# Experts of a small mixture-of-experts layer summed feature-major instead of token-major, with routing coefficients spread through DRAM

## The reference, cut to what matters

```python
xn = layernorm(x)
logits = xn @ router_w + router_b + load_balancer          # 4 experts
rw, sel = top_k(logits, 2); rw = softmax(rw)
e0 = silu(xn @ sw_w1) * (xn @ sw_w3) @ sw_w2               # 128 -> 512 -> 128
e1 = gelu(sym(xn) @ me_c1w + me_c1b) @ me_c2w + me_c2b     # 128 -> 256 -> 128
h2 = layer_norm(syn + attn); ff = relu(h2 @ ce_f1w + ..) @ ce_f2w + ..
e2 = layer_norm(h2 + ff) @ ce_gen_w + ce_gen_b
e3 = gelu(xn @ ml_w1 + ml_b1) @ ml_w2 + ml_b2              # 128 -> 512 -> 128
out = x + attention(xn) + sum over the two chosen experts of rw * e
```

## Time and profile before

| | us |
|---|---|
| median of 3 runs | 510.76 (510.4 to 511.81) |
| the profiled execution | 510.39 |
| its span, first to last instruction | 508.3 |
| PE busy | 487.1 (96%) |
| DVE busy | 402.1 (79%) |
| ACT busy | 231.0 (45%) |
| POOL busy | 172.9 (34%) |

### The profile page before, as it was taken

How to read it: one execution, slowest core, us unless ns; L and a number is a source line. 1 busy time by engine, 2 the same in 40 slices (tenths; PEclk the granted TensorE clock), 3 DMA queues, 4 the chain that set the end, 5 groups by cost and what they waited for, 6 DMA issues and landing times.

```text
span 508.3 us, 9640 instructions
## 1 busy us (share of the span) xinstructions
PE 487.1 (96%) x3072; PEld 425.5 (84%) x3072; DVE 402.1 (79%) x1339; ACT 231.0 (45%) x413; POOL 172.9 (34%) x310
## 2 busy tenths in 40 slices
PE   3779999999999999999999999999999999999995
PEld 2559898898989889898988989898898989889894
DVE  5997886868788686878968687896868789695875
ACT  3452634626363462636346263634626363462621
POOL 5351433415243341524334152432415243240320
PEclk9989999999999999999999999999999999999998
DMA  6000001010100101010010101001010100100000
GB/s 244 3 1 21 3 1 43 2 43 0 43 0 0 41 0 41 0 41 0 0 41 0 41 0 41 0 0 41 0 41 0 41 0 0 41 2 23 0 22 21
DMA packets 17921, 11.21 MB, mean 22 GB/s; under 512 B 752, under 2 KB 17264, under 8 KB 17904
## 3 DMA queue, kind: packets, MB, share of 16 engines
q1 hardware_dynamic: 17616, 10.85, 7.1%
q10 hardware_dynamic: 288, 0.15, 0.1%
HBM read 6.80 MB, written 4.19 MB: 22 GB/s over the span
## 4 chain that ended last, share of the span: by engine, by line
PE 92%; DVE 5%; DMA 1%; issue 0%; ACT 0%; DVEq 0%; SPq 0%
PE EX L901 22%; PE S L935 12%; PE S L937 11%; PE S L936 11%; PE ATT L991 7%; PE EX L913 6%; PE S L944 5%; PE EX L921 3%; PE S L975 2%; PE S L1012 1%; PE S L1010 1%; PE S L1011 1%; DMA W<-weights 1%; PE TR L972 1%; PE S L1026 1%; PE TR L858 1%
## 5 line engine op out<-in xcount | busy, mean ns | idle before, releaser
L935 PE MATMUL S<-xh,WH 128*128 128x512 f32 x224 | 94.5, 422 | 2.5 <-DVE pr L724 1.8
L937 PE MATMUL S<-xh,WL 128*128 128x512 f32 x224 | 89.1, 398 | 0.0
L936 PE MATMUL S<-xl,WH 128*128 128x512 f32 x224 | 88.8, 396 | 0.0
L901 PEld LDWEIGHTS EX<-W,hid 128*128 128x128 f32 x512 | 59.7, 192 | 1.4
L401 POOL TENSOR_TENSOR hidl<-hid,hidh 128x512 fp32r<-128x512 f32 x32 | 40.8, 1295 | 56.8 <-ACT hidh L487 56.8
L901 PE MATMUL EX<-scaled,hid 128*128 128x128 f32 x512 | 59.8, 275 | 0.0
L901 PE MATMUL EX<-W,hid 128*128 128x128 f32 x512 | 59.8, 274 | 0.0
L901 PEld LDWEIGHTS EX<-scaled,hid 128*128 128x128 f32 x512 | 58.5, 192 | 0.1
L935 PEld LDWEIGHTS S<-xh,WH 128*128 128x128 f32 x224 | 42.4, 189 | 18.1 <-DVE gate L730 5.7
L361 POOL TENSOR_TENSOR veps_x<-mv_x,eps 128x4 f32<-128x4 f32 x16 | 3.3, 205 | 153.9 <-DVE mv_x L518 153.9
L652 DVE SCALAR_TENSOR_TENSOR OUT<-EX,coef,OUT 128x128 f32<-128x128 f32 x192 | 53.8, 344 | 1.3 <-PE EX L913 0.2
(11 more groups left out here) (166 smaller groups left out, 945.2 us busy)
## 6 DMA issues: line engine op xcount, KB each, us to landing
X<-x SPq DMA_DIRECT2D x16, 256.0 KB, 2.9
out<-OUT SPq DMA_DIRECT2D x16, 256.0 KB, 2.3
W<-weights SPq DMA_DIRECT2D x1, 768.0 KB, 9.2
W<-weights SPq DMA_DIRECT2D x1, 512.0 KB, 8.1
W<-weights SPq DMA_DIRECT2D x1, 418.5 KB, 7.3
W<-weights SPq DMA_DIRECT2D x1, 384.0 KB, 8.6
W<-weights SPq DMA_DIRECT2D x1, 320.5 KB, 8.1
ROW<-rows ACTq DMA_DIRECT2D x1, 133.0 KB, 5.3
```

The lines of the kernel that those rows point to most:

```text
L901: ins = pe.matmul(EX[EX_BANK[e]][:, t, :], hid[e][:, j, t * P:(t + 1) * P], weight[:, j * P:(j + 1) * P], start=(e == 0 and j == 0), stop= ...
L935: pe.matmul(bank[:, :], wh, hi, start=True, stop=False)
L936: pe.matmul(bank[:, :], wh, lo, start=False, stop=False)
L937: pe.matmul(bank[:, :], wl, hi, start=False, stop=True).then_inc(unit_ready, 1)
```

## The change

Expert results are now feature-major like the first products. Each second product (`expert`, `expert2`) is a float32r triple per 128 hidden features, so the weights sw_w2 (halved), me_c2w, ml_w2 and the folded gen_w are split too, and the hidden tiles of experts 0, 1 and 3 as well as u need high halves (ACT) and low halves (POOL for experts 3, 2 and 0, DVE for expert 1 and u). The `tok` tiles take a split form as well (TH, TL), eight matmuls with the high half of x, then four with its low half. The copy xT is gone.

A coefficient now belongs to a column, not to a partition. POOL computes the coefficients (`weigh`), SP writes them to DRAM (`kept`, 128 x 16 elements) and reads them back with every partition receiving all 2048 of them (`share`, 8 KB per partition, 1 MB). The inverse deviation of u times coefficient 2 goes the same way (`kept_u`, `share_u`, 2 KB per partition). DVE sums the experts in `acc`, 512 columns at a time, with the bias of an expert as a scalar per partition; PE turns acc back (`turn_back`), and one DVE operation adds it to OUT (`finish`). The ranking works in the bank TR with fewer semaphore steps.

```diff
+        acc = [sb(f"acc{k}", [P, T]) for k in range(2)]
+        share = [sb(f"share{k}", [P, P, NT, E]) for k in range(2)]
+        share_u = sb("share_u", [P, P, NT])
...
+            def spread_u(g):
+                sp.wait_ge(u_weighed, g.count(1, 1))
+                sp.dma_start(kept_u[g.par], u_weight[:, :]).then_inc(kept_u_stored, DMA_INC)
+                sp.wait_ge(kept_u_stored, g.count(DMA_INC, DMA_INC))
+                sp.dma_start(share_u[:, :, :], kept_u[g.par:g.par + 1].broadcast_to([P, P, NT])) \
+                    .then_inc(share_u_loaded, DMA_INC)
+            def spread(g):
+                sp.wait_ge(coef_ready, g.count(1, 1))
+                sp.dma_start(kept[g.par], coef[g.par][:, :, :].rearrange("p t e -> p (t e)")) \
+                    .then_inc(kept_stored, DMA_INC)
+                sp.wait_ge(kept_stored, g.count(DMA_INC, DMA_INC))
+                sp.dma_start(share[g.par][:, :, :, :].rearrange("p q t e -> p q (t e)"),
+                             kept[g.par:g.par + 1].broadcast_to([P, P, NT * E])).then_inc(share_loaded, DMA_INC)
             def turn(g, first, last):
                 if not first:
-                    store(g.prev())
+                    spread_u(g.prev())
+                spread(g)
                 if two_more(g):
                     sp.wait_ge(att_added, g.count(1, 1))
                     load_x(Group(g.pair, g.off + 2))
+                if not first:
+                    store(g.prev())
...
+            def weigh(g):
+                pool.wait_ge(tlean_ready, g.count(1, 1))
+                pool.tensor_tensor(turned[:, :, :], tlean[:, :, :], half[:, :, :], ALU.mult)
+                pool.drain()
+                pool.tensor_tensor(coef[g.par][:, :, :], turned[:, :, :], half[:, :, :], ALU.add) \
+                    .then_inc(coef_ready, 1)
...
-                pool.wait_ge(hid_high, g.count(1, 1))
-                for j in range(2):
-                    pool.tensor_tensor(hidl[:, j, :], hid[2][:, j, :], hidh[:, j, :], ALU.subtract) \
-                        .then_inc(hid_low, 1)
+                low(3, 0, 2)
+                low(3, 2, 4)
+                weigh(g)
+                low(2, 0, 2)
+                low(0, 0, 2)
+                low(0, 2, 3)
+                low(0, 3, 4)
...
-                act.copy(xT[g.par][:, :], TR[:, :])
                 act.copy(xh[g.par][:, :], TR[:, :]).then_inc(x_high, 1)
...
                 half_gate(1)
+                high(3, 0, 2, "c1")
+                high(3, 2, 4, "c3")
...
+            def scale(g, n, e):
+                dve.wait_ge(ex_ready, g.count(E, n))
+                bank = EX[EX_BANK[e]][:, :, :]
+                dve.scalar_tensor_tensor(out=bank, in0=bank, scalar=bias[:, e:e + 1], in1=shared(g, e),
+                                         op0=ALU.add, op1=ALU.mult).then_inc(ex_scaled, 1)
+            def expert3(g):
+                dve.wait_ge(share_loaded, g.count(DMA_INC, DMA_INC))
+                dve.wait_ge(ex_ready, g.count(E, 1))
+                dve.scalar_tensor_tensor(out=acc3(g), in0=EX[EX_BANK[3]][:, :, :], scalar=bias[:, 3:4], in1=shared(g, 3),
+                                         op0=ALU.add, op1=ALU.mult).then_inc(ex_taken, 1)
...
+            def finish(g):
+                dve.wait_ge(turned_back, g.count(1, 1))
+                dve.wait_ge(att_added, g.count(1, 1))
+                dve.tensor_tensor(OUT[g.par][:, :, :], EX[1][:, :, :], OUT[g.par][:, :, :], ALU.add) \
+                    .then_inc(out_ready, 1)
...
+            def expert(g, e, parts, col):
+                bank = rows_of(EX[EX_BANK[e]])
+                for j in range(parts):
+                    pe.wait_ge(hid_low[e], g.count(parts, j + 1))
+                    wh, wl = WH[:, col + j * P:col + (j + 1) * P], WL[:, col + j * P:col + (j + 1) * P]
+                    pe.matmul(bank, wh, hidh[e][:, j, :], start=(j == 0), stop=False)
+                    pe.matmul(bank, wh, hidl[e][:, j, :], start=False, stop=False)
+                    ins = pe.matmul(bank, wl, hidh[e][:, j, :], start=False, stop=(j == parts - 1))
+                ins.then_inc(ex_ready, 1)
...
                 if not first:
-                    pe.wait_ge(ex_taken, g.prev().count(E, 4))
-                project(g, 0, "b3", scaled)
+                    pe.wait_ge(out_ready, g.prev().count(1, 1))
+                expert(g, 0, 4, SPLIT["sw2"])
```

More of the change, by code:

```diff
@@ L143, in build @@
         me_b = sb("me_b", [P, 2])
[L144 to L149, removed]
+        bias = sb("bias", [P, E])
+        turned = sb("turned", [P, NT, E])
         minus1 = sb("minus1", [P, NT])
@@ L327, in turn, with tail @@
                     load_x(Group(g.pair, g.off + 2))
-            turns(sp, turn, store)
+                if not first:
+                    store(g.prev())
+            def tail(g):
+                spread_u(g)
+                store(g)
+            turns(sp, turn, tail)
             for k in range(2):
@@ L460, in half_gate, with high @@
                     a, _ = unit(f"a{j}")
-                    act.activation(th[:, j, :], a[:, :], ACT.Tanh, scale=0.5).then_inc(th_ready, 1)
+                    act.activation(th[:, j % 2, :], a[:, :], ACT.Tanh, scale=0.5).then_inc(th_ready, 1)
+                def high(e, a, b, unit_name):
+                    act.wait_ge(released[g.bank(unit_name)], g.uses_before(unit_name) + 1)
+                    act.copy(hidh[e][:, a:b, :], hid[e][:, a:b, :]).then_inc(hid_high[e], 1)
                 act.wait_ge(qk_ready, g.count(1, 1))
@@ L718, in turn @@
                 ins.then_inc(c_stats, 1)
+                if not first:
+                    u_combine(g.prev())
                 def masked_scores():
@@ L748, in turn @@
                     fold_first()
-                if not first:
-                    expert0(g.prev())
-                    u_combine(g.prev())
+                else:
+                    split_hid1(g.prev())
                 dve.wait_ge(h2_high, g.count(1, 1))
@@ L792, in turn @@
                     fold_last()
+                else:
+                    scale(g.prev(), 3, 1)
+                    add(g.prev(), 3, 1)
+                    expert2(g.prev())
                 silu(2)
-                dve.wait_ge(tlean_ready, g.count(1, 1))
-                route(dve.scalar_tensor_tensor(out=coef[g.par][:, :, :], in0=tlean[:, :, :], scalar=1.0,
-                                               in1=half[:, :, :], op0=ALU.add, op1=ALU.mult))
-                assert rs[0] == ROUTE_STEPS
                 silu(3)
+                expert3(g)
                 if not first:
-                    expert2_add(g.prev())
+                    finish(g.prev())
+                if two_more(g):
+                    x_moments(Group(g.pair, g.off + 2))
                 f2, free = unit("f2")
@@ L803, in turn @@
                                          op0=ALU.add, op1=ALU.add).then_inc(free, 1)
-                dve.wait_ge(att_added, g.count(1, 1))
-                for t in range(NT):
-                    ins = dve.scalar_tensor_tensor(out=OUT[g.par][:, t, :], in0=row("me_c2b"),
-                                                   scalar=coef[g.par][:, t, 1:2], in1=OUT[g.par][:, t, :],
-                                                   op0=ALU.mult, op1=ALU.add)
-                ins.then_inc(bias1_added, 1)
                 if not last:
                     x_low(g.next())
-                dve.wait_ge(bias1_added, g.count(1, 1))
-                mix(g, 1, 3)
-                if two_more(g):
-                    x_moments(Group(g.pair, g.off + 2))
+                split_u(g)
+                scale(g, 2, 0)
+                add(g, 2, 0)
             def tail(g):
@@ L819, in tail @@
                 u_combine(g)
-                expert0(g)
-                expert1(g)
-                expert2_scale(g)
-                expert2_add(g)
+                split_hid1(g)
+                scale(g, 3, 1)
+                add(g, 3, 1)
+                expert2(g)
+                finish(g)
             turns(dve, turn, tail)
```

337 lines of the change are left out of this document (185 added, 152 removed).

## The result

The changed kernel takes 527.11 us (median of 4, 525.14 to 528.81) against 510.69 beside it: ratio 1.0326, 95% interval 1.0293 to 1.0359. It is slower. I had forecast 507 us in a range of 494 to 524.

What follows compares the result with a forecast made beforehand. PE bound the kernel at 29.68 us a turn; the new chain through DRAM would set 29.3. From 510.4, 5.5 less in the turns, 1.5 less at the start and 3.7 more at the end gave 507.1; 80% range 494 to 524.

Steps and rivals of the forecast that it cites:

- PE's own work: PE's work in a turn: 1.80 us less, leaving 27.87, with twelve 260-column `tok` matmuls at 1.56 in all.
- rival A: Transfers come earlier than reckoned and the engines' own orders bound: period some 28.4 us, 493 in all; chance 0.20.
- Steps 1 to 5: Chain from expert 0's matmuls through u's moments, tanh, ACT's cast, POOL's low halves, coefficients at 22.26 us, then `kept`, 1.5.
- Step 6: SP's `share` load of 1.05 MB: 4.0 us, with 2.45 for the bytes, 0.96 ahead and 0.6 behind.
- Step 7: DVE's expert 3 addition and `finish`, 0.69 us each, with hops 1.45; PE may start the next expert 0 at 29.31.
- Rival B: Round trip through DRAM slower, 6.7 us with the hop: period 30.4, 523.4 in all; chance 0.27.
- rival C: Strided reads cost DVE 0.53 us more each, so it reaches expert 3's addition late: period 30.0, 518.7 in all; chance 0.17.
- The start: First turn, with no `finish` before it and less PE work: 1.5 us less (bounds 2.5 less, 1 more).
- The end: Behind the last moments of u, with the `kept_u` and `share_u` trip: about 12.5 us against 8.8, 3.7 more.
- a margin of 0.15 us a turn: Period must stay under 29.53 us, 0.15 below 29.68, to pay for the net 2.2 of start and end.

Runs made afterwards that it cites:

- rows: late_xfirst with the coefficients turned on PE and copied by ACT, so DVE reads `share` at consecutive addresses: 501.82 us, ratio 0.9823.
- contig: The changed kernel with `share` and `share_u` read at consecutive addresses, so coefficients belong to wrong tokens and experts: 520.07 us, ratio 1.0184.
- small: The changed kernel with `share` and `share_u` filled once, each turn's broadcast bringing only 16 and 4 elements per partition: 499.75 us, ratio 0.9797.
- late_xfirst: The changed kernel with x loaded before the coefficient transfers and expert 3's addition behind `finish`, x's moments, u and low halves: 502.62 us, ratio 0.9862.
- after_start: The changed kernel with POOL's two added weight splits put off in the first turn to behind expert 3's low halves: 523.28 us, ratio 1.0261.
- xfirst: The changed kernel with SP loading x of the group two ahead before the coefficient transfers: 525.88 us, ratio 1.0312.
- best: late_xfirst with the coefficients as in rows, weight splits put off in the first turn and u turned early in the last: 496.34 us, ratio 0.9717.

## Why the prediction was wrong

**PE's own work.** Busy time went down as forecast, and the matmuls of 260 columns come 0.12 to 0.13 apart where nothing holds them. In all they take 2.05 us (267.50 to 269.55) and not 1.56: for 0.44 of it in each turn a weight load waits for the moments of u. Against that the transpositions take 0.35 to 0.36 and not 0.43 to 0.44. So the sum of 27.87 us in a turn is about right by errors that cancel. In rows the period is 28.56, a little over the 28.4 of rival A; there A's bound holds, in the changed kernel it does not.

**Steps 1 to 5** held, in the turn shown: 4.96 us to the moments (forecast 4.95), 10.45 to tanh's end (10.56), 1.01 to POOL (1.15), 5.58 to the coefficients' end (5.60), 1.46 to share's issue (1.60, with the 0.1 between the two transfers).

**Step 6 failed in size.** From share's issue to DVE's operation it is 4.73 us in the mean of 14 turns, and not 4.0. The shown turn is a short one, 4.32; it sums to 29.54. The term that was mis-sized is the time of the bytes: I had put 2.45 us, from the 428 GB/s of the earlier trace rows, and 1.56 around them. In the last turn the bytes take 2.8 us, at 372 GB/s, with 1.46 around them. In 12 of the 16 turns they also nearly stop soon after they began, as in the fifth window above, and in one they begin half a microsecond late. The three turns with neither are the three short ones, 4.26 to 4.32; the others take 4.6 to 5.05. Why the bytes stop stays open.

**Step 7 failed in size.** I took the strided operation at a plain one's 0.69. It is 1.09, and the step 1.74 to 1.76 instead of 1.45. contig shows 0.34 of it to be the stride.

Rival B thus came true at part of its price (6.2 us from the coefficients' end to DVE's operation where it had 6.7), and of rival C only the longer operation on the chain; that DVE comes to it too late, C's mechanism, did not: DVE waits there. I had held the two for alternatives. In the mean of the 14 turns behind the first period 29.31 + 0.73 for step 6 + 0.29 for step 7 - 0.30 for what steps 1 to 5 took less gives the 30.03 measured; with the first period the mean is 30.10, and the turns lose 6.4 us instead of gaining 5.5. small and contig show both terms; late_xfirst shows that it was the chain.

**The start failed as a mechanism.** Forecast 1.5 us less, measured 1.6 more, and another 1.1 by which the first period is longer than the others. I said that the first turn has no `finish` before it, but its u stands behind expert 3's addition, which waits 2.32 us for `share` (u at 52.24 against 48.56 before). And POOL's two splits, which I had priced only as POOL's time within a bound of 1 us, hold DVE up: after_start is worth 3.3 us. How much that costs varies. In contig and xfirst the held copy_predicated takes 3.14 and 3.15 us, PE comes back at 34.11 and 34.47, the granted clock is 0.50 from 34 to 42 us, and the first moments come at 59.1 and 59.4. The changed kernel's profiled execution, with 56.0, is the fastest of its four, 2.0 us under the median.

**The end failed in size.** 7.0 more instead of 3.7 (its terms add up to 12.35, not 12.5, so 3.55). `share_u` took 3.55 from its issue at 513.26 to DVE's operation, not 2.4; its copy 1.86, not 1.6; POOL's root and weight 2.4, not 1.65; DVE's read 1.05; and PE, idle for 6.67 us, turned back in 1.11 us at a granted clock of 0.50, where the turns have 0.60.

The forecast had stood on a margin of 0.15 us a turn from which B decides. B alone, at 523, was inside the range; the misses of the turns, the start and the end together lie 3 us beyond its upper end.

## What to carry to other kernels

When a change sends a value round through DRAM, price the trip from the nearest load's whole landing time, and then ask not how long it is but what stands in the waiting engine's queue behind the wait: here moving one operation behind `finish`, the moments of x, u and its splits, with the load that they need put first, was worth 24 us, and the length of the trip then cost nothing. Add up rivals that lie on one chain; they are not alternatives. Look at the first and last turn apart, for what is hidden in between is bare there: some 6 us of the best kernel's gain came from two edits that run once.

## What the runs showed of the hardware

- Operations of DVE in float32 over 512 columns of PSUM, in place or not, with the second input from SBUF: scalar_tensor_tensor takes 1.09 to 1.12 us in the mean where that input steps 64 bytes and 0.75 at consecutive addresses (contig, rows), tensor_tensor 1.05 to 1.08 at 16 bytes and 0.69 at consecutive ones (contig). The larger step costs no more than the smaller.
- One row of DRAM to all 128 partitions takes 2.8 us for 8 KB in all, 3.9 to 4.1 for 256 KB and 4.5 to 4.8 for 1 MB, from issue to landing; a plain 256 KB load 2.8 to 2.9, but 5.1 when it is issued behind the 1 MB. An 8 KB store takes 1.4.
- The 1 MB of such a broadcast moved at 372 GB/s where nothing interrupted it (2.8 us), and in 12 of 16 turns it dropped to between 0 and 66 GB/s for a quarter to half a microsecond, soon after its start.
- DVE's copy_predicated and tensor_scalar from SBUF to SBUF were held up by POOL's subtractions, copy_predicated by two in a row, up to 3.15 us instead of 0.42 (xfirst); not by POOL's rstd_x.
- After 6.67 us of idleness PE ran at a granted clock of 0.50, 1.2 GHz. Behind waits of 2.20 and 1.45 us in the first turn the same stretch of work had 0.72 and 0.73. Behind the waits of 1.33 and 0.85 us in the turn shown above it stayed at 1.00.
